# Layer-norm tiles before attention: each tile's PSUM evacuation issued after the next tile's Ln and Exp

## The chip, the cores and the metric

The kernel runs on all 8 cores of one Trainium2 chip, each with its own share of the rows and no exchange between cores. The metric is the device time of the slowest core in microseconds (us).

## What is computed

One transformer-like layer over x of shape 16 x 2048 x 1024 (batch, sequence, width), float32:

```python
x = x + layernorm(attention(layernorm(x), w_q, w_k, w_v, w_u, b_u))   # 16 heads of 64, causal
x = x + layernorm(ffn(layernorm(x), ...))    # a gated recurrence over the 16 batches, then tanh
```

`layernorm` subtracts the mean over the 1024 columns and divides by sqrt(variance + 1e-5); it has no weights. Attention needs K and V of all 2048 rows of a batch, and Q of the core's own rows only.

## The kernel before

Each core owns 256 of the 2048 rows of every batch (16 strips of 16 rows). For each of the 16 batches it computes the layer norm, K and V of the whole sequence, and Q, scores, softmax and output for its own 256 rows. After all batches the FFN part loads and transposes its weights, normalises the core's rows, runs the recurrence over the batches, and writes y.

The program is written by hand as one list of operations for each engine (class `Plan`): `P.op(engine, ...)` appends an instruction, `P.wait(engine, semaphore, value)` makes that engine wait at this place of its list, and `inc` raises a semaphore when an instruction ends. An engine works through its list in order, so the order in which the Python code calls `P.op` is the order on the engine.

A batch begins with the layer-norm stage: 16 tiles of 128 rows from xg (the whole sequence) into lnf, and then 2 tiles from xm (the core's own rows) into lnm, which is the buffer of. Each is one call of `emit_ln_tile_bf` (line 226). For tile k:

- SyncE loads the tile (512 KB) into a slot, once GpSimd has finished with that slot's last tile (lines 233 to 235). There are 4 slots for the xg tiles (two xt buffers, ex and of) and 2 for the xm tiles (the xt buffers).
- VectorE computes mean and variance (lines 242 to 248).
- ScalarE computes 1/sqrt(variance + eps) as Ln and then Exp (lines 251 and 254).
- GpSimd normalises the tile into lt or x1, in turn (line 258). It waits until TensorE has transposed the tile of two calls ago.
- TensorE transposes it in eight 128x128 pieces into one half of the PSUM buffer PA, in turn (line 265). It waits until the half's last tile has been evacuated.
- ScalarE copies that half as bfloat16 into lnf or of (line 272): the evacuation, counted by the semaphore ve_Tevac.

After the last tile of a batch TensorE waits for all evacuations (line 362) and starts the K projection (line 373), 32 groups of 8 matmuls, and then V (line 390), Q (line 416) and the attention proper. The two waits with a lag of one are these, as the code has them:

```python
P.wait("gpsimd", "te_T", max(P.v("te_T") - 1, 0))
P.wait("tensor", "ve_Tevac", max(P.v("ve_Tevac") - 1, 0))
```

`P.v` is the count of the increments written so far, at the place in the Python code where it is called.

Of the kernel before, what the change touches and what calls it, by code (L numbers as in the profile page):

```python
# [79 lines left out]
def _apof(buf):  # L80
    return buf.ap() if hasattr(buf, "ap") and callable(getattr(buf, "ap")) \
        else buf


def sub3(buf, off, d1, d2):
    a = _apof(buf)
    return bass.AP(a.tensor, a.offset + off, [[a.ap[0][0], a.ap[0][1]], d1, d2])
# [135 lines left out]
    return nm, rs  # L223


def emit_ln_tile_bf(P, B, src_dram_ap, k, dst_fm, dst_col, slots):
    nslot = len(slots)
    par4 = k % nslot
    par2 = k % 2
    xt = slots[par4]  # L230
    lt = B["lt"] if par2 == 0 else B["x1"]
    PA = B["PA"]
    P.wait("sync", "gp_lnapply", max(P.v("gp_lnapply") - (nslot - 1), 0))
    P.dma("sync", lambda sy: sy.dma_start(out=xt, in_=src_dram_ap),
          inc=f"ldx{par4}")
    P.wait("vector", "gp_lnapply", max(P.v("gp_lnapply") - (nslot - 1), 0))
    P.wait("vector", f"ldx{par4}")
    bnb, mv, nm, rs = (B["bnb"][par4], B["mv"][par4], B["nm"][par4],
                       B["rs"][par4])

    def stats(v):
        v.bn_stats(bnb[:, 0:6], xt[:, 0:512])  # L242
        return v.bn_stats(bnb[:, 6:12], xt[:, 512:1024])
    P.op("vector", stats, inc="ve")
    P.wait("vector", "ve")
    P.op("vector", lambda v: v.bn_aggr(mv[:], bnb[:]), inc="ve")
    P.wait("vector", "ve")
    P.op("vector", lambda v: v.tensor_scalar(nm[:], mv[:, 0:1], -1.0, None,
                                             ALU.mult), inc="ve")
    P.wait("scalar", "ve")  # L250
    P.op("scalar", lambda sc: sc.activation(rs[:], mv[:, 1:2], AF.Ln,
                                            bias=B["eps"][:, 0:1]), inc="se")
    P.wait("scalar", "se")
    P.op("scalar", lambda sc: sc.activation(rs[:], rs[:], AF.Exp, scale=-0.5),  # L254
         inc="ve_rs")
    P.wait("gpsimd", "ve_rs")
    P.wait("gpsimd", "te_T", max(P.v("te_T") - 1, 0))
    P.op("gpsimd", lambda g, lt=lt: g.tensor_scalar(  # L258
        lt[:], xt, nm[:, 0:1], rs[:, 0:1], ALU.add, ALU.mult),
        inc="gp_lnapply")  # L260
    P.wait("tensor", "gp_lnapply")
    P.wait("tensor", "ve_Tevac", max(P.v("ve_Tevac") - 1, 0))
    po = 1024 * par2
    for ch in range(8):
        P.op("tensor", lambda t, ch=ch, po=po, lt=lt: t.transpose(  # L265
            PA[:, po + 128 * ch: po + 128 * (ch + 1)],
            lt[:, 128 * ch:128 * (ch + 1)], B["identf"][:]),
            inc="te_T" if ch == 7 else None)
    P.wait("scalar", "te_T")
    stride = dst_fm.shape[1] // 8  # L270
    P.op("scalar", lambda sc, po=po, dst_col=dst_col, dst_fm=dst_fm, stride=stride:
         sc.copy(  # L272
             sub3(dst_fm, dst_col, [stride, 8], [1, 128]),
             sub3(PA, po, [128, 8], [1, 128])),
         inc="ve_Tevac")


def emit_ln_tile(P, B, src_dram_ap, par, dst_fm, dst_col, lt2=False):
# [35 lines left out]
def emit_attention(P, B, cfg):  # L314
    NB = DEBUG_NB or cfg["NB"]
    units = cfg["units"]
    xg, xm = cfg["xg"], cfg["xm"]
    lnf, kf, va, qf, ex, of = (B["lnf"], B["kf"], B["va"], B["qf"], B["ex"],
                               B["of"])
    wq, wk, wv, wu = B["wq"], B["wk"], B["wv"], B["wu"]  # L320
    PA, PB = B["PA"], B["PB"]
    lnm = lnf if cfg["lnm_is_lnf"] else B["lnm"]
    masks = B["masks"]

    for name, arena in (("wq", wq), ("wk", wk), ("wv", wv), ("wu", wu)):
        dram = cfg[name]
        for dmc in range(8):
# [6 lines left out]
          inc="ld_mask")  # L334
# [3 lines left out]
    for b in range(NB):  # L338
# [6 lines left out]
        if cfg.get("al_on_ex"):  # L345
# [6 lines left out]
            P.wait("sync", "st_al0")  # L352
            P.wait("sync", "st_al1")
        slots = cfg["ln_slots"]
        for tt in range(NKT):
            emit_ln_tile_bf(P, B, xg[b, 128 * tt:128 * (tt + 1), :], tt,
                            lnf, 128 * tt, slots)
        if not cfg["lnm_is_lnf"]:
            for tt in range(cfg["NQ"] // 128):
                emit_ln_tile_bf(P, B, xm[b, 128 * tt:128 * (tt + 1), :], tt,  # L360
                                lnm, 128 * tt, slots[0:2])
        P.wait("tensor", "ve_Tevac")
        P.wait("vector", "gp_lnapply")
        if DEBUG_STAGE == "ln1":
# [2 lines left out]
        for g4 in range(4):  # L367
            for hp in range(8):
                par = (g4 * 8 + hp) % 2
                po = 512 * par  # L370
                P.wait("tensor", "ve_kevac", max(P.v("ve_kevac") - 1, 0))
                for dmc in range(8):
# [5 lines left out]
                        inc="te_k" if dmc == 7 else None)  # L378
# [5 lines left out]
        for kt in range(NKT):  # L384
            par = kt % 2
            po = 1024 * par
            P.wait("tensor", "gp_vrepack", max(P.v("gp_vrepack") - 1, 0))
            for dmc in range(8):
                for hf in range(2):
# [6 lines left out]
                        inc="te_v" if (dmc == 7 and hf == 1) else None)  # L396
# [4 lines left out]
                inc="gp_vrepack")  # L401
# [6 lines left out]
        for unit in units:  # L408
# [3 lines left out]
            for hp in range(8):  # L412
                P.wait("tensor", "ve_qevac")
                for dmc in range(8):
# [8 lines left out]
                         inc="te_q" if dmc == 7 else None)  # L423
# [10 lines left out]
            for quad in range(4):  # L434
# [24 lines left out]
                for idx, (i, vs, d_lo, d_w) in enumerate(ktl):  # L459
                    slot = 1024 * (idx % 2)  # L460
                    P.wait("tensor", "se_exp", max(P.v("se_exp") - 1, 0))
                    for hq in range(4):
# [10 lines left out]
                             inc="te_s" if hq == 3 else None)  # L473
                    if d_w:
                        for hq in range(4):
# [8 lines left out]
                                 inc="te_s" if hq == 3 else None)  # L484
# [19 lines left out]
                for j in range(2):  # L504
# [5 lines left out]
                        inc="te_bc" if j == 1 else None)  # L510
# [5 lines left out]
                for hq in range(4):  # L516
# [6 lines left out]
                        inc="ve_norm")  # L523
# [3 lines left out]
            for st in range(2):  # L527
                po = 1024 * st
# [8 lines left out]
                for j in range(2):  # L537
# [5 lines left out]
                        inc="te_up" if j == 1 else None)  # L543
# [272 lines left out]
def build_attn_program(version):  # L816
# [17 lines left out]
    with ctx:  # L834
        B = alloc_common(nc, ctx, need_attn=True, need_ffn=False)
        B["masks"] = ctx.enter_context(
            nc.sbuf_tensor("masks_sb", [128, 8 * mask_w], BF16))
        P = Plan(nc, ctx)
        blk = ctx.enter_context(nc.Block())
        cfg = {  # L840
            "NB": NB, "NQ": NQ, "units": make_units(version),
            "xg": xg, "xm": None, "lnm_is_lnf": True,
            "wq": wq, "wk": wk, "wv": wv, "wu": wu, "bu": bu,
            "masks_dram": masks_dram, "mask_w": mask_w,
            "aln_dst": lambda b, r0: aln[b, r0:r0 + 128, :],
        }
        emit_setup(P, B)
        emit_attention(P, B, cfg)
        P.run(blk)
# [34 lines left out]
def build_fused_program():  # L884
# [20 lines left out]
    with ctx:  # L905
# [27 lines left out]
        })  # L933
        emit_setup(P, B)
        emit_attention(P, B, cfg_a)
        for eng in ENGINES:
            P.wait(eng, "st_al0")
# [100 lines left out]
```

## Time and profile before

| | us |
|---|---|
| median of the 2 timed runs | 7825.04 (7629.27 and 8020.81) |
| the profiled execution | 7630.95 |
| its span on the slowest core (core 5) | 7629.1 |
| spans of the 8 cores | 7609.1 to 7629.1 |
| batch 1: GpSimd's first tile to first K matmul | 416.13 to 509.79 |
| busy: PE, DVE, ACT, POOL | 62%, 29%, 19%, 5% |

PE is TensorE's matmuls, PEld its weight loads, DVE VectorE, ACT ScalarE, POOL GpSimd, SPq SyncE's queue, which issues the loads. L272 is line 272 of the kernel. Busy shares are means over stages of different kinds: the 16 batches take up to about 5490 us, the FFN part the rest.

### The profile page before, as it was taken

The page shows a single profiled execution, that of the slowest core. Times are in us where ns is not written, and L with a number is a line of the kernel's source. Part 1 is how long each engine was busy: PE and PEld are TensorE (multiplying, and loading weights), DVE is VectorE, ACT ScalarE, POOL GpSimd, SP SyncE. Part 2 cuts the span into 40 slices and gives each one's busy share as a digit, 9 for nine tenths or more (in the row PEclk, how much of TensorE's full clock was granted, in tenths as well). Part 3 has the DMA queues.
Part 4 walks back from the last instruction along what each step waited for, and adds up shares of the span by engine and source line. Part 5 has one row for each costly group of instructions (what it writes and reads, how often), then busy time and mean ns, then how long its engine had stood idle before and what let it go on. Part 6 is the DMA issues. An engine that isn't in the chain of part 4 may idle for free.

```text
span 7629.1 us, 84840 instructions; the slowest of 8 cores (7609.1 to 7629.1 us)
## 1 busy us (share of the span) xinstructions
PE 4743.2 (62%) x31972; PEld 3005.3 (39%) x31972; DVE 2205.7 (29%) x3874; ACT 1480.4 (19%) x2697; POOL 419.4 (5%) x367
## 2 busy tenths in 40 slices
PE   2856757585766758585775748586633216999322
PEld 1534344343434344343434434343411115888110
DVE  1232323222232322223232222223222233333334
ACT  1212130312212031221213031221200001222222
POOL 3010100101010000101010010101000010000000
PEclk9867768686877768686776868687755557999666
DMA  4010110101010010101011010101011221000222
GB/s 94 1 53 18 36 39 14 53 1 53 1 53 28 25 48 6 53 1 53 17 36 40 14 53 1 53 1 53 20 66 66 80 88 48 12 15 9 80 92 92
DMA packets 95066, 299.11 MB, mean 39 GB/s; under 512 B 14800, under 2 KB 14800, under 8 KB 94672
## 3 DMA queue, kind: packets, MB, share of 16 engines
q1 hardware_dynamic: 90000, 285.30, 11.3%
q0 software_dynamic: 4672, 8.39, 0.7%
q8 instruction: 267, 4.37, 0.2%
q14 instruction: 127, 1.04, 0.0%
HBM read 268.49 MB, written 33.55 MB: 40 GB/s over the span
## 4 chain that ended last, share of the span: by engine, by line
PE 56%; DVE 11%; issue 10%; ACT 10%; DMA 6%; POOL 5%; SPq 1%; ACTq 0%; DVEq 0%; POOLq 0%
PE PA L373 12%; PE PB L390 12%; PE PA L265 7%; PE PB L688 4%; PE PB L451 4%; PE PB L677 4%; ACT ex L487 3%; PE PB L416 3%; PE PA L467 2%; POOL x_ L258 2%; POOL lt L258 2%; PE PA L584 2%; DVE of L519 1%; PE PB L758 1%; PE PA L531 1%
## 5 line engine op out<-in xcount | busy, mean ns | idle before, releaser
L487 ACT ACTIVATE ex<-PA 128x1024 bf16<-128x1024 f32 (+15 forms) x1024 | 624.3, 624 | 2683.4 <-PE PA L477 2640.6
L373 PE MATMUL PA<-lnf,wk_sb 128*128 128x512 bf16 x4096 | 919.6, 389 | 22.2 <-ACT of L272 22.2
L390 PE MATMUL PB<-wv_sb,lnf 128*128 128x512 bf16 x4096 | 886.7, 379 | 0.0
L265 PE MATMUL PA<-identf,lt 128*128 128x128 f32 x1152 | 279.2, 424 | 723.0 <-POOL lt L258 644.9
L373 PEld LDWEIGHTS PA<-lnf,wk_sb 128*128 128x128 bf16 x4096 | 407.7, 100 | 532.6 <-issue 71.9
L451 PE MATMUL PB<-ex,va 128*65 128x256 bf16 (+15 forms) x4096 | 483.6, 243 | 208.2 <-ACT ex L487 131.2
L390 PEld LDWEIGHTS PB<-wv_sb,lnf 128*128 128x128 bf16 x4096 | 400.8, 98 | 483.3
L265 PE MATMUL PA<-identf,x_ 128*128 128x128 f32 x1152 | 279.3, 424 | 473.1 <-POOL x_ L258 473.1
L380 DVE CAST kf<-PA 128x512 bf16<-128x512 f32 x512 | 354.1, 692 | 707.0 <-PE PA L373 707.0
L265 PEld LDWEIGHTS PA<-identf,lt 128*128 128x128 f32 x1152 | 225.6, 223 | 777.5 <-issue 777.5
L467 PE MATMUL PA<-qf,kf 128*128 128x256 bf16 (+15 forms) x4096 | 515.2, 256 | 22.0 <-DVE qf L427 22.0
L398 DVE CAST va<-PB 128x1024 bf16<-128x1024 f32 x256 | 314.1, 1227 | 578.5 <-PE PB L390 578.5
L272 ACT CAST lnf<-PA 128x1024 bf16<-128x1024 f32 x256 | 259.1, 1012 | 1003.2 <-PE PA L265 1003.2
L265 PEld LDWEIGHTS PA<-identf,x_ 128*128 128x128 f32 x1152 | 225.7, 223 | 526.6 <-issue 526.6
L512 DVE CAST rb<-PB 64x1024 bf16<-64x1024 f32 x64 | 77.9, 1217 | 1162.1 <-PE PB L505 1162.1
L451 PEld LDWEIGHTS PB<-ex,va 128*65 128x65 bf16 x4096 | 304.5, 118 | 254.8 <-issue 238.4
L758 PE MATMUL PB<-wv_sb,va 128*128 128x512 bf16 x512 | 151.1, 468 | 374.0 <-DMA va<-ln2s 371.3
L584 PE MATMUL PA<-identf,xt 128*128 128x128 f32 x512 | 168.8, 433 | 333.3 <-DVE lnf L590 38.3
L467 PEld LDWEIGHTS PA<-qf,kf 128*128 128x128 bf16 x4096 | 329.1, 108 | 103.0 <-issue 67.8
L242 DVE BATCH_NORM_STATS2 bnb<-xt 128x6 f32<-128x512 f32 x160 | 111.1, 694 | 722.8 <-DMA xt<-xg 425.0
L258 POOL TENSOR_SCALAR lt<-xt,nm,rs 128x1024 f32<-128x1024 f32 x80 | 95.7, 1196 | 3995.2 <-ACT rs L254 3995.2
L416 PE MATMUL PB<-of,wq_sb 128*128 128x256 bf16 x1024 | 212.6, 378 | 151.8 <-DVE qf L427 125.0
(99 smaller groups left out, 4900.2 us busy)
## 6 DMA issues: line engine op xcount, KB each, us to landing
xt<-xg SPq DMA_DIRECT2D x128, 512.0 KB, 3.9
xt<-xm SPq DMA_DIRECT2D x96, 512.0 KB, 4.6
ex<-xg SPq DMA_DIRECT2D x64, 512.0 KB, 3.9
of<-xg SPq DMA_DIRECT2D x64, 512.0 KB, 3.9
va<-alns SPq DMA_DIRECT2D x64, 256.0 KB, 4.5
va<-ln2s SPq DMA_DIRECT2D x32, 512.0 KB, 3.7
y<-lt SPq DMA_DIRECT2D x32, 512.0 KB, 3.0
alns<-ex SPq DMA_DIRECT2D x32, 256.0 KB, 2.0
```

The lines of the kernel that those rows point to most:

```text
L258: P.op("gpsimd", lambda g, lt=lt: g.tensor_scalar(lt[:], xt, nm[:, 0:1], rs[:, 0:1], ALU.add, ALU.mult), inc="gp_lnapply")
L265: P.op("tensor", lambda t, ch=ch, po=po, lt=lt: t.transpose(PA[:, po + 128 * ch: po + 128 * (ch + 1)], lt[:, 128 * ch:128 * (ch + 1)], B[" ...
L373: P.op("tensor", lambda t, dmc=dmc, hp=hp, g4=g4, po=po: t.matmul(PA[:, po:po + 512], wk[:, 1024 * dmc + 128 * hp: 1024 * dmc + 128 * (hp ...
L380: P.op("vector", lambda v, hp=hp, g4=g4, po=po: v.tensor_copy(kf[:, 2048 * hp + 512 * g4: 2048 * hp + 512 * (g4 + 1)], PA[:, po:po + 512]) ...
L390: P.op("tensor", lambda t, dmc=dmc, kt=kt, hf=hf, po=po: t.matmul(PB[:, po + 512 * hf: po + 512 * (hf + 1)], lnf[:, 2048 * dmc + 128 * kt: ...
L398: P.op("vector", lambda v, po=po, kt=kt: v.tensor_copy(sub3(va, 1040 * kt, [65, 16], [1, 64]), sub3(B["PB"], po, [64, 16], [1, 64])), inc= ...
L416: src_stride=src_stride: t.matmul(PB[:, 1792:2048], wq[:, 1024 * dmc + 128 * hp: 1024 * dmc + 128 * (hp + 1)], lnm[:, src_stride * dmc + q ...
L451: last=(idx == nkt_u - 1): t.matmul(PB[0:65, 256 * hq + vs: 256 * (hq + 1)], va[:, 1040 * i + 65 * h: 1040 * i + 65 * (h + 1)], sub2(ex, 1 ...
L467: lambda t, i=i, vs=vs, hq=hq, hp=hp, qo=qo, slot=slot: t.matmul(PA[:, slot + 256 * hq + vs: slot + 256 * (hq + 1)], kf[:, 2048 * hp + 128 ...
L487: P.op("scalar", lambda s, vs=vs, slot=slot, idx=idx: s.activation(sub3(ex, 1024 * (idx % 2) + vs, [256, 4], [1, 256 - vs]), sub3(PA, slot ...
L584: P.op("tensor", lambda t, ic=ic, oc=oc: t.transpose(PA[:, 128 * oc:128 * (oc + 1)], B["xt"][oc][:, 128 * ic: 128 * (ic + 1)], identf[:]), ...
L677: par=par, first=(ic == 0 and gi in (0, 2)): t_.matmul(PB[:, doff:doff + 256], B[wT][:, 1024 * ic + 128 * mc: 1024 * ic + 128 * (mc + 1)], ...
```

## The change

`emit_ln_tile_bf` no longer writes tile k's evacuation at its end; it returns it as a function, and the call for tile k+1 writes it right after that tile's Exp. The last one of a batch is written after the loops. On ScalarE the order was Ln k, Exp k, evacuation k, Ln k+1, ...; it becomes Ln k, Exp k, evacuation k-1, Ln k+1, Exp k+1, evacuation k, and so on. The instructions themselves and the buffers are the same.

```diff
-def emit_ln_tile_bf(P, B, src_dram_ap, k, dst_fm, dst_col, slots):
+def emit_ln_tile_bf(P, B, src_dram_ap, k, dst_fm, dst_col, slots, pend=None):
...
     P.op("scalar", lambda sc: sc.activation(rs[:], rs[:], AF.Exp, scale=-0.5),
          inc="ve_rs")
+    if pend is not None:
+        pend()
     P.wait("gpsimd", "ve_rs")
...
-    P.wait("scalar", "te_T")
-    stride = dst_fm.shape[1] // 8
-    P.op("scalar", lambda sc, po=po, dst_col=dst_col, dst_fm=dst_fm, stride=stride:
-         sc.copy(
-             sub3(dst_fm, dst_col, [stride, 8], [1, 128]),
-             sub3(PA, po, [128, 8], [1, 128])),
-         inc="ve_Tevac")
+
+    def evac():
+        P.wait("scalar", "te_T")
+        stride = dst_fm.shape[1] // 8
+        P.op("scalar",
+             lambda sc, po=po, dst_col=dst_col, dst_fm=dst_fm, stride=stride:
+             sc.copy(
+                 sub3(dst_fm, dst_col, [stride, 8], [1, 128]),
+                 sub3(PA, po, [128, 8], [1, 128])),
+             inc="ve_Tevac")
+    return evac
...
+        pend = None
         for tt in range(NKT):
-            emit_ln_tile_bf(P, B, xg[b, 128 * tt:128 * (tt + 1), :], tt,
-                            lnf, 128 * tt, slots)
+            pend = emit_ln_tile_bf(P, B, xg[b, 128 * tt:128 * (tt + 1), :],
+                                   tt, lnf, 128 * tt, slots, pend)
         if not cfg["lnm_is_lnf"]:
             for tt in range(cfg["NQ"] // 128):
-                emit_ln_tile_bf(P, B, xm[b, 128 * tt:128 * (tt + 1), :], tt,
-                                lnm, 128 * tt, slots[0:2])
+                pend = emit_ln_tile_bf(P, B, xm[b, 128 * tt:128 * (tt + 1), :],
+                                       tt, lnm, 128 * tt, slots[0:2], pend)
+        if pend is not None:
+            pend()
         P.wait("tensor", "ve_Tevac")
```

evac()'s wait on te_T names a value when it is called: inside the call for tile k+1 and ahead of that tile's transposes, so it is the count up to tile k's own.

## Rows read from the trace of the kernel before

**Rows 1.** The page's chain that ended last, by line.
```profile
PE PA L373 12%; PE PB L390 12%; PE PA L265 7%; PE PB L688 4%; PE PB L451 4%; PE PB L677 4%; ACT ex L487 3%; PE PB L416 3%; PE PA L467 2%; POOL x_ L258 2%; POOL lt L258 2%; PE PA L584 2%; DVE of L519 1%; PE PB L758 1%; PE PA L531 1%
```

**Rows 2.** One window: length, busy us of PE, PEld, DVE, ACT, POOL; clock; DMA.
```profile
416.00:510.00 94.00, 35.11 (x145) 28.35 (x146) 27.91 (x68) 24.97 (x52) 21.48 (x18) 0.50 0.28 86
```

**Rows 3.** The evacuation's line over the whole run: count, shortest, median, longest ns.
```profile
L272 ACT CAST lnf<-PA x256: 1012/1012/1013, 80.1 to 5245.7; 128x1024 bf16<-128x1024 f32 x128
L272 ACT CAST of<-PA x32: 1012/1012/1012, 163.7 to 5256.2; 128x1024 bf16<-128x1024 f32 x32
```

**Rows 4.** Timeline, batch 1, one tile: start, us, instruction, idle before and releaser.
```profile
419.61 1.01 ACT L272 CAST lnf<-PA 128x1024 bf16<-128x1024 f32 x1 [3.71 <-PE PA L265]
...
420.52 0.30 ACT L251 ACTIVATE rs<-mv,eps 128x1 f32<-128x1 f32 x1
420.90 0.20 ACT L254 ACTIVATE rs<-rs 128x1 f32<-128x1 f32 x1
...
421.34 1.19 POOL L258 TENSOR_SCALAR x_<-xt,nm,rs 128x1024 f32<-128x1024 f32 x1 [4.01 <-ACT rs L254]
...
422.78 1.94 PE L265 MATMUL PA<-identf,x_ 128*128 128x128 f32 x8 [3.27 <-POOL x_ L258]
...
424.81 1.01 ACT L272 CAST lnf<-PA 128x1024 bf16<-128x1024 f32 x1 [3.71 <-PE PA L265]
...
426.55 1.19 POOL L258 TENSOR_SCALAR lt<-ex,nm,rs 128x1024 f32<-128x1024 f32 x1 [4.01 <-ACT rs L254]
```

**Rows 5.** Timeline, head of batch 1: the first tiles' statistics, the first Ln and normalise.
```profile
413.36 0.69 DVE L242 BATCH_NORM_STATS2 bnb<-xt 128x6 f32<-128x512 f32 x1 [7.04 <-DMA xt<-xg]
...
415.31 0.29 ACT L251 ACTIVATE rs<-mv,eps 128x1 f32<-128x1 f32 x1 [10.79 <-DVE nm L248]
...
415.89 0.69 DVE L242 BATCH_NORM_STATS2 bnb<-xt 128x6 f32<-128x512 f32 x1 [0.68 <-DMA xt<-xg]
416.13 1.19 POOL L258 TENSOR_SCALAR lt<-xt,nm,rs 128x1024 f32<-128x1024 f32 x1 [249.54 <-ACT rs L254]
...
417.77 0.69 DVE L242 BATCH_NORM_STATS2 bnb<-ex 128x6 f32<-128x512 f32 x1
```

**Rows 6.** Loads in batch 1: one load and its reader, landings, the window of four.
```profile
427.81 0.33 SPq L234 DMA_DIRECT2D ex<-xg  x1
...
431.71 0.69 DVE L242 BATCH_NORM_STATS2 bnb<-ex 128x6 f32<-128x512 f32 x1 [3.24 <-DMA ex<-xg]
...
DMA to landing us min/median/max: 3.6/3.8/8.5
...
412.00:416.00 4.00, 0.00 (x0) 0.00 (x0) 1.75 (x5) 0.50 (x2) 0.00 (x0) 0.50 1.01 281
```

**Rows 7.** Timeline, tail of batch 1: tile 14, the xm loads, last evacuation, K.
```profile
489.06 1.19 POOL L258 TENSOR_SCALAR lt<-ex,nm,rs 128x1024 f32<-128x1024 f32 x1 [4.01 <-ACT rs L254]
490.33 5.53 SPq L234 DMA_DIRECT2D xt<-xm  x2
...
494.23 0.69 DVE L242 BATCH_NORM_STATS2 bnb<-xt 128x6 f32<-128x512 f32 x1 [13.82 <-DMA xt<-xm]
...
508.43 1.01 ACT L272 CAST of<-PA 128x1024 bf16<-128x1024 f32 x1 [3.98 <-PE PA L265]
...
509.79 50.43 PE L373 MATMUL PA<-lnf,wk_sb 128*128 128x512 bf16 x220 [1.73 <-ACT of L272]
```

**Rows 8.** Timeline, batch 0: GpSimd on its second tile, and the K start.
```profile
81.79 1.19 POOL L258 TENSOR_SCALAR x_<-xt,nm,rs 128x1024 f32<-128x1024 f32 x1 [42.15 <-ACT rs L254]
...
170.02 10.16 PE L373 MATMUL PA<-lnf,wk_sb 128*128 128x512 bf16 x37 [1.25 <-ACT of L272]
```

**Rows 9.** Windows at the K start, PE only: length, busy (count), clock, DMA.
```profile
508.00:512.00 4.00, 2.27 (x7) 0.50 0.01 2
512.00:516.00 4.00, 4.00 (x12) 0.57 0.00 0
516.00:520.00 4.00, 4.00 (x20) 1.00 0.00 0
```

## What I expected, and why

> **What bounds the kernel now.** I read the page's chain first, then asked the trace which stretches that chain runs through, and then read one such stretch instruction by instruction. The chain by lines is led by matmuls of the K and V projections, but line 265 (the layer-norm transposes) stands third, and both forms of line 258 (GpSimd's normalise) are on it too [rows 1]. These lines exist in one stage only: the layer norm at the head of each batch. The window over one such stage shows what is to be seen there: of 94 us, TensorE is busy 35, VectorE 28, ScalarE 25, GpSimd 21 and the DMA engines 28% [rows 2]. No engine is near its limit, so the stage is bound by a chain that goes from engine to engine. It has 18 tiles a batch, 288 in all: the evacuation of line 272 ran 256 times into lnf and 32 times into of [rows 3].
>
> One tile, read in order of time [rows 4]: the evacuation of the tile before starts on ScalarE at 419.61; Ln follows at 420.52 (0.91 later), Exp at 420.90 (0.38), GpSimd's normalise at 421.34 (0.44), the eight transposes at 422.78 (1.44), and the next evacuation at 424.81 (2.03). That sums to 5.20 us and closes on itself, for GpSimd starts again at 426.55, 5.21 after 421.34. The evacuation sat idle 3.71 us before it started, waiting for TensorE. Ln of the next tile stands behind it in ScalarE's program, although VectorE had that tile's statistics long before: those of the tile that GpSimd starts at 426.55 were begun at 417.77 [rows 4, 5]. So each tile passes through all five stations before the next one may begin, and the stage costs 5.2 us a tile.
>
> **The change, part by part.** No instruction is added or removed. The evacuation of tile k-1 moves behind Ln and Exp of tile k on ScalarE; the last one of a batch is issued after the loop. The waits of the other engines keep their values: when tile k's own waits are written, the evacuations counted are again those up to k-1, so TensorE waits for evacuation k-2 (the half of PA it will overwrite), and GpSimd for the transposes of k-2 (the lt or x1 buffer it will overwrite). With both buffers in pairs, tile k no longer needs tile k-1.
>
> Steady state: evacuation k-1 is followed on ScalarE by Ln k+1, Exp k+1, GpSimd k+1, TensorE k+1, evacuation k+1. These are the same five steps, 0.91 + 0.38 + 0.44 + 1.44 + 2.03 = 5.20 us, but they now carry the chain forward by two tiles: 2.60 us a tile, if no engine is full before that. TensorE needs 1.94 us a tile [rows 4], ScalarE 0.91 + 0.38 + 0.20 = 1.5, GpSimd 1.2, VectorE 1.88 (from 415.89 to 417.77, two tiles' statistics back to back [rows 5]). All fit in 2.60. GpSimd and VectorE already run side by side in these rows with unchanged durations, so I put their overlap at nothing; the new overlap, an evacuation reading one half of PA while TensorE writes the other, I put at nothing too. The nearest row is the K projection, where VectorE reads one half of PA while TensorE writes the other and 20 matmuls still fall in 4 us at the full clock [rows 9]. Were the evacuation 10% longer by it, the nine two-tile steps of a batch would cost 0.9 us, 14 us in all; that is my upper bound, and below nothing there is no reason for a gain.
>
> Loads: a tile's slot is refilled four tiles ahead. Line 258 of tile k-4 starts, 1.26 later SyncE issues the load (426.55 to 427.81), and VectorE starts on it 3.90 after that (431.71) [rows 4, 6]; Ln can start 1.95 after the statistics begin (413.36 to 415.31 [rows 5]). Together 7.11 us after GpSimd's start on k-4. The new schedule wants that Ln at 2 x 5.21 - 0.82 = 9.60 us. So a load has 2.5 us to spare: it may take 6.4 us where it takes 3.90. The demand rises from one 512 KB load in 5.2 us to one in 2.6, about 200 GB/s; when four loads were queued at the head of the batch, the engines moved 281 GB/s at a share of 1.01 [rows 6], which is 1.87 us for one. The spacing of 2.6 is longer than that, so loads don't queue up. I take 3.90. The bounds are 3.6, the shortest landing of the batch, and 8.5, the longest, seen behind three others [rows 6].
>
> Head of the batch: tile 0 is unchanged, GpSimd at 416.13 [rows 5]. Tile 1's statistics begin at 415.89, so its Ln starts at 417.84 and GpSimd at 418.66, where it was 421.34. Evacuation 0 runs at 419.61 as before, and tile 2 follows at 421.34. Even tiles thus start at 416.13 + 5.21 j, tile 14 at 452.6 instead of 489.06 [rows 7]: 36.46 us earlier. Odd tiles run 2.52 behind the even ones.
>
> Tail: the two tiles from xm use only two slots, so their loads are issued late. Call T the start of GpSimd on tile 14. The load of the first is issued at T + 1.27 and its statistics begin at T + 5.17 (489.06, 490.33, 494.23 [rows 7]). In the old order that was hidden. Now Ln is wanted at T + 4.38 and can start only at T + 5.17 + 1.95 = 7.12: a stall of 2.7 us on ScalarE, with the evacuation of tile 15 queued behind it. That evacuation then runs at about T + 7.7 and ends before the transposes that need its half of PA, at T + 11.9, so it costs nothing more. The second load is issued after tile 15, at T + 2.52 + 1.27 = 3.79; statistics 7.69, Ln 9.64, GpSimd 10.46, transposes 11.90, evacuation 13.93. The first K matmul came 1.36 after the last evacuation (508.43 to 509.79), and that evacuation ran 0.28 later than the pattern; with both it starts at T + 15.57, where before it was T + 20.73. That gives 5.16 us.
>
> A batch gains 36.46 + 5.16 = 41.6 us of 93.7 (416.13 to 509.79). Batch 0 waits for weights until 78 us, but its second tile starts GpSimd at 81.79 and the first K matmul comes at 170.02 [rows 8]; in the new order it is tile 2 that starts there, tile 14 comes six steps later at 113.1 and K at 128.7: 41.3. The FFN stages have their own tile code and are not touched. 16 x 41.6 = 666 us. From the profiled execution's own 7630.95 us this gives **6965 us**. The median shown, 7825.04, is that of two runs at 7629.27 and 8020.81; my sum stands against the lower. Were the new kernel's median to lie 2.5% above its profiled execution in the same way, it would read 7142, which my range holds.
>
> **TensorE's clock.** In this stage the granted clock is 0.50, the level of 1.2 GHz, with TensorE busy 35 of 94 us on transposes alone [rows 2]. At the K projection's start it is still 0.50, then 0.57, and 1.00 from 516 on; the windows hold 7, 12 and then 20 matmuls in 4 us [rows 9]. From 509.79 to 516 some 30 could have run, 17 did, so the cold start costs about 2.6 us a batch. In the new order TensorE would be busy 1.94 of each 2.6 us. I leave the clock as it is, because all transposes seen in this stage ran at 0.50. The Trainium skill (TensorE: Matmul & The Clock Gate, Part 4: PE-mode transpose) says that transposes do not count as activity for the clock; by that rule the sum stays at 6965. The same page's Part 1 says that activity in general releases the throttle; if transposes did count, it would be the second rival below. The trace agrees with the first at 37% busy; no run here yet shows 75%.
>
> **Rivals.**
> *Loads become the bound.* If eight cores asking for twice the rate bring every load to 8.5 us, four tiles take 1.26 + 8.5 + 1.95 + 0.82 = 12.53 us instead of 10.41. Tiles 6, 10 and 14 each lose 2.12 (6.4 together), and the tail, where two slots serve, about 4.0: a batch gains 31.2, and the time is 7631 - 499 = 7132. For it: the queue of four loads did show 8.5. Against it: they were issued within 2 us, and three tiles' time between loads is now left free. 12%.
> *TensorE's clock rises.* Transposes would at best take half, 0.97 less in each two-tile step: seven steps and the tail are 7.8, with the K start 10.4 us a batch, so 6965 - 166 = 6799. For it: twice the density. Against it: nothing in the trace shows the transposes' duration at another clock, nor the clock rising under them. 10%.
> *It doesn't separate the tiles.* If some wait still tied tile k to k-1, the period would stay 5.2 and the time 7631. The pairs of buffers and the wait values speak against it. 4%.
> *Slower: head-of-line blocking on ScalarE.* Evacuation k now stands behind Ln k+1, which needs a load that the evacuation doesn't. The ScalarE queue is served in order, as the row at 420.52 right behind 419.61 shows. This loses once four tiles take more than 4 x 5.2 us, that is once a load takes over 20.8 - 4.0 = 16.8 us; at 20 us the 18 tiles would take 108 us for 94, and the time would be about 7631 + 16 x 14.5 = 7860. The longest load on record is half of the threshold. 2%.
>
> **How the numbers follow.** My forecast, 6965, holds 72%; by itself it spans 6920 (a K start without the cold matmuls) to 7020 (loads of 6.5 us, which add 2.6 in each tail, 42 in all, and the 14 us of the overlap). The range is 6880 to 7150: up to the load-bound case, down to half way to the case of the raised clock, which leaves out 16%. A difference of about 2% is what a measurement of this kernel can tell from none. All cases but the last two are faster by over 2%: faster 0.94, same 0.04, slower 0.02.
>
> **What would show it.** In the new profile, GpSimd's starts in a batch should alternate at 2.5 and 2.7 us; the evacuation's row should show an idle time well under 3.71; Ln and Exp should stand ahead of it; the first K matmul should come about 52 us after GpSimd's first tile. VectorE's wait for xt<-xm should appear on ScalarE as a wait of Ln, near 2.7 us. Landings much over 6.4 us, or VectorE as ScalarE's releaser in every tile, would mean the loads bind. Clock rows over 0.50 in the stage, or transposes under 1.94 us for eight, would mean the second rival. A spacing of 5.2 would mean that I overlooked a wait.

## The result, and the profile after

| | before | changed |
|---|---|---|
| median, us | 7943.36 (10 runs, 7629.27 to 8113.69) | 7077.54 (13 runs, 6943.50 to 7435.96) |
| runs with every core at its usual clock, us | 7629 to 7633 | 6943 to 6948 |
| ratio of these | | 0.9101, 95% interval 0.9083 to 0.9119 |

Some executions on this chip have four or eight cores at a lower granted clock and take some per cent longer, whatever the kernel, so the ratio goes by the others, and rows are always those of a core at its usual clock. For the changed kernel that is core 5, which is also the core of the rows before; its span is 6927.5 us where it was 7629.1. A second profile of the changed kernel (e11_again, below) gave 6947.8 for the same core.

The timeline of core 5 in batch 1, in the steady part (start, us, instruction, idle before and releaser), answers to [rows 4]:

```profile
404.77 1.19 POOL L260 TENSOR_SCALAR x_<-xt,nm,rs 128x1024 f32<-128x1024 f32 x1 [1.57 <-ACT rs L254]
...
405.48 1.01 ACT L277 CAST lnf<-PA 128x1024 bf16<-128x1024 f32 x1 [0.94 <-PE PA L267]
...
406.21 1.94 PE L267 MATMUL PA<-identf,x_ 128*128 128x128 f32 x8 [0.83 <-POOL x_ L260]
...
406.39 0.30 ACT L251 ACTIVATE rs<-mv,eps 128x1 f32<-128x1 f32 x1
...
406.78 0.20 ACT L254 ACTIVATE rs<-rs 128x1 f32<-128x1 f32 x1
407.21 1.19 POOL L260 TENSOR_SCALAR lt<-ex,nm,rs 128x1024 f32<-128x1024 f32 x1 [1.25 <-ACT rs L254]
408.25 1.01 ACT L277 CAST lnf<-PA 128x1024 bf16<-128x1024 f32 x1 [1.27 <-PE PA L267]
...
409.98 1.19 POOL L260 TENSOR_SCALAR x_<-of,nm,rs 128x1024 f32<-128x1024 f32 x1 [1.57 <-ACT rs L254]
```

GpSimd's starts are 2.44 and 2.77 us apart, two of them 5.21, where one took 5.21 before. The evacuation waits 0.9 to 1.3 us for TensorE instead of 3.71. Over the run its two rows, which answer to [rows 3], show an idle time of 301.5 + 43.4 us where it was 1003.2 + 120.1 (groups of ScalarE's instructions, core 5: count, busy us, mean ns, idle before; L272 is the evacuation in the kernel before, L277 in the changed one):

```profile
L272 ACT CAST lnf<-PA 128x1024 bf16<-128x1024 f32 x256 | 259.1, 1012 | 1003.2 <-PE PA L265 1003.2
L251 ACT ACTIVATE rs<-mv,eps 128x1 f32<-128x1 f32 x288 | 85.5, 297 | 148.4 <-DVE nm L248 148.3
...
L272 ACT CAST of<-PA 128x1024 bf16<-128x1024 f32 x32 | 32.4, 1012 | 120.1 <-PE PA L265 120.1
...
L277 ACT CAST lnf<-PA 128x1024 bf16<-128x1024 f32 x256 | 258.8, 1011 | 301.5 <-PE PA L267 301.2
L251 ACT ACTIVATE rs<-mv,eps 128x1 f32<-128x1 f32 x288 | 85.5, 297 | 234.0 <-DVE nm L248 233.9
...
L277 ACT CAST of<-PA 128x1024 bf16<-128x1024 f32 x32 | 32.4, 1012 | 43.4 <-PE PA L267 43.4
```

The evacuation waits 778 us less in all. Ln (L251) waits 86 us more for VectorE's statistics, 234.0 for 148.4 (3.96 us in the tail of batch 1 alone, below). The difference, 693 us, is close to what the stages became shorter by, 685 us (below).

The same timeline at the tail of batch 1 answers to [rows 7]:

```profile
407.21 1.19 POOL L260 TENSOR_SCALAR lt<-ex,nm,rs 128x1024 f32<-128x1024 f32 x1 [1.25 <-ACT rs L254]
...
408.48 3.09 SPq L234 DMA_DIRECT2D xt<-xm  x2
...
413.71 0.69 DVE L242 BATCH_NORM_STATS2 bnb<-xt 128x6 f32<-128x512 f32 x1 [6.91 <-DMA xt<-xm]
...
415.66 0.29 ACT L251 ACTIVATE rs<-mv,eps 128x1 f32<-128x1 f32 x1 [3.96 <-DVE nm L248]
...
416.16 0.99 ACT L277 CAST lnf<-PA 128x1024 bf16<-128x1024 f32 x1
...
416.48 1.19 POOL L260 TENSOR_SCALAR lt<-xt,nm,rs 128x1024 f32<-128x1024 f32 x1 [5.31 <-ACT rs L254]
...
421.83 1.01 ACT L277 CAST of<-PA 128x1024 bf16<-128x1024 f32 x1 [0.86 <-PE PA L267]
...
423.09 2.10 PE L382 MATMUL PA<-lnf,wk_sb 128*128 128x512 bf16 x9 [1.63 <-ACT of L277]
```

The first xm load is issued 1.27 us after GpSimd's start on tile 14, and Ln waits 3.96 us for its statistics: the stall that the prediction put at 2.7. The evacuation at 416.16 is that of tile 15: it stands behind this Ln and Exp in ScalarE's list, 2.8 us after its transposes had ended (at 413.36), and it costs nothing, as the prediction had it.

From such timelines I read, for each of the 16 batches, when GpSimd starts on tiles 0, 14, 16 and 17 and when the first K matmul starts. The table gives means over batches 1 to 15 in us (tile 16 is the first xm tile). "Fast" is how many of a batch's 18 groups of eight transposes took under 1.5 us. Rows are of core 5, but of core 1 for e1_xm4, core 0 for e2_before_xm4 and core 2 for e7_fill4. Between cores and between executions of one kernel the column "0 to K" differs by about 0.4 us: core 0 of the kernel before has 94.09, and core 5 in e11_again 51.18.

| kernel | tile 0 to 14 | 14 to 16 | 14 to K | 0 to K | fast |
|---|---|---|---|---|---|
| before | 73.15 | 10.45 | 20.50 | 93.65 | 0 |
| changed | 35.01 | 8.09 | 15.76 | 50.77 | 2.7 |
| predicted | 36.47 | 7.94 | 15.57 | 52.0 | 0 |
| e1_xm4 | 35.25 | 5.16 | 12.40 | 47.64 | 2.7 |
| e2_before_xm4 | 73.26 | 10.48 | 20.88 | 94.14 | 0 |
| e3_tied | 43.51 | 7.99 | 16.16 | 59.67 | 0 |
| e4_depth2 | 30.91 | 4.53 | 10.78 | 41.70 | 8.7 |
| e5_slots2 | 55.86 | 8.01 | 16.51 | 72.36 | 0 |
| e6_before_slots2 | 73.15 | 10.46 | 20.48 | 93.63 | 0 |
| e7_fill4 | 32.94 | 7.81 | 15.15 | 48.09 | 15.3 |
| e8_depth2_s8 | 26.65 | 3.81 | 9.73 | 36.38 | 14.2 |
| e10_before_fill4 | 66.08 | 9.20 | 18.29 | 84.37 | 11.0 |

The whole sum closes on this table: core 5 spends 1536.5 us from tile 0 to K in the 16 batches before, 851.4 after, 685.1 less; the 15 stretches from a K start to the next tile 0 give another 11 (245.51 to 244.75 each); together 696 of the 701.6 by which its span fell. Nothing was given back elsewhere. In e11_again the same core spends 857.6 us from tile 0 to K, 679 less than before, and 245.80 in each stretch between: the gain in the stages repeats, the 11 us outside them doesn't.

### The profile page after: what moved, and what is told of

Its sections match the earlier page's. It is cut to its first block, busy times and chain, and to the rows that moved or that the text cites. A ratio compares the mean times of both kernels' runs of the same rounds, so it can differ in the third digit from the quotient of the medians.

```text
span 7069.1 us, 84840 instructions; the slowest of 8 cores (6927.5 to 7069.1 us)
## 1 busy us (share of the span) xinstructions
PE 4839.7 (68%) x31972; PEld 3022.9 (43%) x31972; DVE 2205.7 (31%) x3874; ACT 1485.6 (21%) x2697; POOL 420.0 (6%) x367
## 4 chain that ended last, share of the span: by engine, by line
PE 58%; DVE 13%; ACT 9%; issue 8%; DMA 8%; POOL 3%; SPq 1%; DVEq 0%; ACTq 0%; POOLq 0%
PE PA L382 14%; PE PB L399 13%; PE PB L697 5%; PE PB L460 5%; PE PB L686 4%; PE PA L267 4%; ACT ex L496 3%; PE PB L425 3%; PE PA L476 3%; PE PA L593 2%; PE PA L540 1%; DVE of L528 1%; PE PB L767 1%; POOL x_ L260 1%; DMA xt<-xg 1%
## 5 line engine op out<-in xcount | busy, mean ns | idle before, releaser
L382 PE MATMUL PA<-lnf,wk_sb 128*128 128x512 bf16 x4096 | 973.2, 405 | 22.0 <-ACT of L277 22.0
L399 PE MATMUL PB<-wv_sb,lnf 128*128 128x512 bf16 x4096 | 946.5, 397 | 0.0
L267 PE MATMUL PA<-identf,lt 128*128 128x128 f32 x1152 | 256.8, 398 | 463.9 <-POOL lt L260 372.9
L267 PEld LDWEIGHTS PA<-identf,lt 128*128 128x128 f32 x1152 | 208.4, 209 | 515.3 <-issue 515.3
L277 ACT CAST lnf<-PA 128x1024 bf16<-128x1024 f32 x256 | 258.8, 1011 | 307.9 <-PE PA L267 307.6
L644 PE MATMUL PA<-identf,lt 128*128 128x128 f32 x256 | 62.1, 424 | 314.5 <-POOL lt L637 314.5
```

Of the source, the lines that this page charges most:

```text
L267: P.op("tensor", lambda t, ch=ch, po=po, lt=lt: t.transpose(PA[:, po + 128 * ch: po + 128 * (ch + 1)], lt[:, 128 * ch:128 * (ch + 1)], B[" ...
L382: P.op("tensor", lambda t, dmc=dmc, hp=hp, g4=g4, po=po: t.matmul(PA[:, po:po + 512], wk[:, 1024 * dmc + 128 * hp: 1024 * dmc + 128 * (hp ...
L399: P.op("tensor", lambda t, dmc=dmc, kt=kt, hf=hf, po=po: t.matmul(PB[:, po + 512 * hf: po + 512 * (hf + 1)], lnf[:, 2048 * dmc + 128 * kt: ...
```

## The experiments

**Is the stall in the tail the late load?** The xm tiles get all four slots, so their loads wait for a tile four back, as the others do.

```diff
-                                       tt, lnm, 128 * tt, slots[0:2], pend)
+                                       tt, lnm, 128 * tt, slots, pend)
```

> The changed kernel, with the two xm tiles loaded under the same rule as the others: the slot is free four tiles back, so the first xm load is issued after tile 12 and not after tile 14. Chain theory (the stall that the changed kernel shows in its tail, 8.1 us from GpSimd's tile 14 to its tile 16 where a steady pair takes 5.2, is the late load): that pair takes 5.2 to 5.3, the first K matmul comes about 13 us after tile 14 instead of 15.8, a gain of 2.5 to 3 us in each of 16 batches, 40 to 48 us, ratio to the kernel before near 0.904. Rival (the tail is bound by ScalarE or by GpSimd, the load only happens to be late as well): no change, ratio 0.910.

Measured: ratio 0.9026 (0.9004 to 0.9048), under the changed kernel's by more than both intervals. Core 1's GpSimd rows at the tail of batch 1:

```profile
409.06 1.20 POOL L260 TENSOR_SCALAR lt<-ex,nm,rs 128x1024 f32<-128x1024 f32 x1 [1.45 <-ACT rs L254]
411.62 1.19 POOL L260 TENSOR_SCALAR x_<-of,nm,rs 128x1024 f32<-128x1024 f32 x1 [1.36 <-ACT rs L254]
414.27 1.19 POOL L260 TENSOR_SCALAR lt<-xt,nm,rs 128x1024 f32<-128x1024 f32 x1 [1.46 <-ACT rs L254]
```

From tile 14 to tile 16 it is 5.21 us, the steady pair, and the stall is gone. The batch gains 3.1 us. The same edit in the kernel before:

> The kernel before, with the same earlier xm loads. Chain theory: in the old order Ln of the first xm tile waited for the evacuation anyway (statistics ready at 496.1, Ln at 498.65), so the load is hidden: ratio 1.00, GpSimd's starts stay 5.2 apart up to the last tile. Rival (late xm loads always cost, before too): about 2.5 us a batch less, ratio 0.995.

Measured: ratio 1.0035 (0.9979 to 1.0092), GpSimd's pair at the tail 10.48 us on core 0, as on core 0 of the kernel before. The late load cost nothing in the old order, and it became a cost only when the chain that hid it was halved.

**Do the two PSUM halves carry the overlap?** TensorE waits for the evacuation just before, not for the one two back.

```diff
-    P.wait("tensor", "ve_Tevac", max(P.v("ve_Tevac") - 1, 0))
+    P.wait("tensor", "ve_Tevac")
```

> The changed kernel, but TensorE waits for the evacuation of the tile just before (as if PA had one half only). Theory that the pair of PSUM halves lets two tiles overlap: from the end of one tile's transposes 0.09 us to the evacuation, 1.0 to 1.4 until TensorE may start, 1.94 for the transposes, so 3.1 to 3.4 us a tile in place of 2.6; 18 tiles cost 9 to 14 us more a batch, 150 to 230 us in all, ratio 0.93 to 0.94. Rival (only ScalarE's order matters, the halves don't): ratio 0.910.

Measured: ratio 0.9304 (0.9273 to 0.9334). The timeline of core 5, batch 1:

```profile
390.00 1.01 ACT L277 CAST lnf<-PA 128x1024 bf16<-128x1024 f32 x1 [1.68 <-PE PA L267]
...
391.15 1.94 PE L267 MATMUL PA<-identf,lt 128*128 128x128 f32 x8 [1.25 <-ACT lnf L277]
...
393.18 1.01 ACT L277 CAST lnf<-PA 128x1024 bf16<-128x1024 f32 x1 [1.69 <-PE PA L267]
...
394.34 1.94 PE L267 MATMUL PA<-identf,x_ 128*128 128x128 f32 x8 [1.25 <-ACT lnf L277]
```

TensorE is now released by the evacuation in each tile, and a tile takes 3.19 us in the steady part: 1.15 from the evacuation's start to the transposes, 1.94 for them and 0.09 back. The order on ScalarE alone gives most of the gain (ratio 0.9304), but not 2.6 us a tile. That takes the wait with a lag of one as well.

**Does the chain's length divide by the number of tiles in it?** Each evacuation is held back by two tiles, on top of e1_xm4 (the end of the batch writes both that are left).

```diff
-    if pend is not None:
-        pend()
+    if pend is not None and len(pend) == 2:
+        pend.pop(0)()
...
-    P.wait("tensor", "ve_Tevac", max(P.v("ve_Tevac") - 1, 0))
+    P.wait("tensor", "ve_Tevac")
...
+    te_val = P.v("te_T")
+
     def evac():
-        P.wait("scalar", "te_T")
+        P.wait("scalar", "te_T", te_val)
```

> As e1_xm4, but each evacuation is held back by two tiles: on ScalarE Ln k, Exp k, evacuation k-2. The five-step chain of 5.2 us then carries three tiles, 1.74 us each, so that another thing binds: VectorE 1.88, TensorE 1.94 at the lower clock, the load path (7.11 + 0.82)/4 = 1.98. Chain theory: 2.0 us a tile, the first K matmul 39 to 41 us after tile 0 instead of 50.8, 150 to 190 us in all, ratio 0.885 to 0.89. Load rival (loads land at 4.5 us or later under this rate): 2.1 to 2.3 a tile, ratio 0.89 to 0.895. Clock rival (denser transposes hold the clock at 1.00): eight transposes take 1.06 and TensorE doesn't bind, VectorE or the loads do, 1.9 to 2.0 a tile, and the K projection starts without cold matmuls.

Measured: ratio 0.8895 (0.8873 to 0.8916). A tile takes 2.2 us (30.91 / 14), the load rival's value, and the rows of core 5 say the same: VectorE waits for the load, and Ln for VectorE.

```profile
376.40 0.69 DVE L242 BATCH_NORM_STATS2 bnb<-xt 128x6 f32<-128x512 f32 x1 [1.30 <-DMA xt<-xg]
...
378.35 0.29 ACT L251 ACTIVATE rs<-mv,eps 128x1 f32<-128x1 f32 x1 [1.67 <-DVE nm L248]
...
378.85 0.99 ACT L279 CAST lnf<-PA 128x1024 bf16<-128x1024 f32 x1
```

The evacuation hardly waits any more, 56.6 + 22.0 us over the run for 301.5 + 43.4, and Ln waits for VectorE 364.6 us for 233.9. The chain moved on from ScalarE's order to the load path. The clock rival holds in part as well: 8.7 of 18 groups of transposes were fast.

**How long is the load path?** Two slots for all tiles, in both kernels.

```diff
-        slots = cfg["ln_slots"]
+        slots = cfg["ln_slots"][0:2]
```

> The changed kernel with two slots for all tiles instead of four, so that a load is issued only after GpSimd has finished the tile two back. Load-path theory (1.26 + 3.9 + 1.95 + 0.82 = 7.93 us from GpSimd's start on tile k-2 to its start on tile k): 3.97 us a tile, tile 14 at 55.5 us after tile 0 (35.0 with four slots), ratio 0.95 to 0.96. Rival (loads are prefetched well enough anyway, ScalarE's chain of 5.2 us for two tiles binds): ratio 0.910.

Measured: ratio 0.9558 (0.9530 to 0.9586), tile 0 to 14 in 55.86 us for 55.5 expected. In the timeline of core 5 the same slot comes round every 7.7 us, with the statistics waiting for the load each time:

```profile
400.67 1.19 POOL L260 TENSOR_SCALAR lt<-xt,nm,rs 128x1024 f32<-128x1024 f32 x1 [4.92 <-ACT rs L254]
...
408.40 1.19 POOL L260 TENSOR_SCALAR lt<-xt,nm,rs 128x1024 f32<-128x1024 f32 x1 [4.00 <-ACT rs L254]
...
413.38 0.69 DVE L242 BATCH_NORM_STATS2 bnb<-xt 128x6 f32<-128x512 f32 x1 [3.08 <-DMA xt<-xg]
...
416.15 1.19 POOL L260 TENSOR_SCALAR lt<-xt,nm,rs 128x1024 f32<-128x1024 f32 x1 [3.74 <-ACT rs L254]
```

> The kernel before with two slots for all tiles. The load path of 7.93 us for two tiles lies under the old chain's 10.4, so the loads stay hidden: GpSimd's starts stay 5.2 apart, ratio 1.00. Together with e5_slots2 it tells that the load path was always there and only the new order uncovers it. Rival (two slots cost by themselves, through contention or issue): a ratio over 1.005 here.

Measured: ratio 0.9994 (0.9932 to 1.0056). With two slots the old order has 10.4 us for a path of 7.9 and loses nothing, the new one has 5.2 and loses 22 us a batch. With four slots the new order leaves the path 10.4 us.

**What does the clock do?** Four matmuls more per tile, which compute nothing that is used.

```diff
             inc="te_T" if ch == 7 else None)
+    for _ in range(4):
+        P.op("tensor", lambda t: t.matmul(
+            B["PB"][:, 0:512], B["wk"][:, 0:128], B["wk"][:, 0:512],
+            start=True, stop=True, skip_group_check=True))
```

> The changed kernel with four extra bf16 matmuls of 512 columns after each tile's transposes, into a part of PB that nothing reads; they only keep TensorE busy (1.7 us a tile at the clock of 0.50, 0.85 at 1.00). Clock theory (the transposes take 1.06 us at the higher level, as the changed kernel shows in some tiles): all tiles after the first two or three take 1.06, a pair of tiles 4.34 instead of 5.21, tile 14 at 31 us instead of 35.0, and the K projection starts without cold matmuls; 5 to 7 us less a batch, ratio 0.895 to 0.90. Rival (the fast transposes come from something else, the clock stays at 0.50 in the stage): TensorE is then busy 3.6 us a tile and binds, 3.6 a tile, ratio 0.945 to 0.95.

Measured, without an interval: the fastest execution took 6883.3 us, 0.902 of the 7625 to 7635 that the kernel before took beside it. In the windows of core 2, batch 1 (length, busy of PE, PEld, DVE, ACT, POOL, granted clock, DMA share, GB/s), the clock rises once and stays:

```profile
376.00:380.00 4.00, 3.23 (x12) 2.38 (x13) 3.43 (x10) 1.70 (x4) 1.71 (x2) 0.50 0.54 143
380.00:384.00 4.00, 4.00 (x22) 3.13 (x22) 2.90 (x7) 1.62 (x5) 1.25 (x2) 0.70 0.60 186
384.00:388.00 4.00, 3.51 (x23) 2.11 (x21) 2.09 (x7) 2.77 (x6) 2.34 (x2) 1.00 0.51 167
```

15 of 18 groups took about 1.06 us, as expected, but tile 0 to 14 fell by 2.1 us only, where I had expected 4, and the ratio is at 0.902 where I had expected 0.895 to 0.90. Some pairs of tiles do take the 4.34 us expected; between them a load is late again, as in e4_depth2, and Ln waits for it (timeline of core 2):

```profile
395.48 0.69 DVE L242 BATCH_NORM_STATS2 bnb<-xt 128x6 f32<-128x512 f32 x1 [1.88 <-DMA xt<-xg]
...
397.43 0.29 ACT L251 ACTIVATE rs<-mv,eps 128x1 f32<-128x1 f32 x1 [1.18 <-DVE nm L248]
```

Would the clock be worth more where nothing else is near? The next one puts the same matmuls into the kernel before:

> The kernel before, its order unchanged, with four extra bf16 matmuls of 512 columns after each tile's transposes, into a part of PB that nothing reads. Clock theory (busier TensorE raises the clock, eight transposes then take 1.06 us and not 1.94, in the old chain too): GpSimd's starts 4.3 us apart instead of 5.2 once the clock is up, about 15 us a batch less and a K start with few cold matmuls, 17 us in all, 270 us over 16 batches, ratio 0.96 to 0.97. Rival (the clock doesn't rise, because TensorE still stands idle between tiles): ratio 1.00, the extra matmuls being hidden in TensorE's 3.27 us of idle time.

Measured, without an interval: the fastest execution took 7445.74 us, 0.976 of the 7627 to 7630 beside it. The rival falls, and the clock theory holds in kind but not in size (0.96 to 0.97 expected): the rise doesn't last. The stage gives 9.3 us a batch, and the stretch from the K start on another 3.6 (241.92 us for 245.51): over the first 7 us of the K projection in batches 1 to 9 the granted clock is 0.81 to 1.00, with 28 to 34 matmuls, where the kernel before has 0.60 to 0.81 and 20 to 27. The windows of core 5, batch 1, with columns as above:

```profile
428.00:432.00 4.00, 1.93 (x12) 1.22 (x12) 1.23 (x4) 1.41 (x3) 0.86 (x2) 1.00 0.44 131
432.00:436.00 4.00, 2.97 (x12) 1.61 (x12) 1.65 (x4) 1.39 (x3) 0.78 (x1) 0.70 0.41 131
436.00:440.00 4.00, 2.44 (x11) 1.99 (x11) 1.65 (x4) 0.29 (x2) 1.19 (x1) 0.50 0.37 106
```

and GpSimd's rows of the timeline over the same stretch:

```profile
427.25 1.19 POOL L258 TENSOR_SCALAR lt<-ex,nm,rs 128x1024 f32<-128x1024 f32 x1 [3.15 <-ACT rs L254]
431.58 1.19 POOL L258 TENSOR_SCALAR x_<-of,nm,rs 128x1024 f32<-128x1024 f32 x1 [3.14 <-ACT rs L254]
436.25 1.19 POOL L258 TENSOR_SCALAR lt<-xt,nm,rs 128x1024 f32<-128x1024 f32 x1 [3.48 <-ACT rs L254]
441.46 1.19 POOL L258 TENSOR_SCALAR x_<-xt,nm,rs 128x1024 f32<-128x1024 f32 x1 [4.01 <-ACT rs L254]
```

With the transposes at 1.06 us, GpSimd starts every 4.33 us, at 1.94 every 5.21. 11 of 18 groups were fast. So the higher level is worth 0.88 us in each step of the chain that holds a group of transposes, in either order.

**Are the loads what binds at a depth of two?** On top of e4_depth2, four more slots, in kf, which is free until the K projection, and eight sets of the small statistics buffers for four.

```diff
+        ln_slots += [B["kf"].ap()[:, 2048 * i:2048 * (i + 1)].bitcast(F32)
+                     for i in range(4)]
```

> As e4_depth2 with eight slots: four more in kf, which is free until the K projection. In e4_depth2 a tile takes 2.2 us and VectorE waits for loads. Load theory: with loads issued eight tiles ahead only their rate counts (1.87 us for 512 KB at 281 GB/s) beside VectorE's 1.88: 1.9 us a tile, tile 14 at 27 us instead of 30.9, 3.5 to 4.5 us less a batch, ratio 0.88 to 0.883. Rival (TensorE at the lower clock, 1.94, or the rate of the loads under all eight cores binds at 2.1 or more): ratio 0.886 to 0.89.

Measured, without an interval: the fastest execution took 6690.85 us, 0.877 of the 7625 to 7635 beside it. Tile 0 to 14 takes 26.65 us, 1.90 a tile, so the load theory holds. GpSimd's starts on core 5 are 1.88 apart, VectorE's time for one tile's statistics:

```profile
379.66 1.20 POOL L260 TENSOR_SCALAR lt<-xt,nm,rs 128x1024 f32<-128x1024 f32 x1 [0.69 <-ACT rs L254]
381.54 1.19 POOL L260 TENSOR_SCALAR x_<-xt,nm,rs 128x1024 f32<-128x1024 f32 x1 [0.68 <-ACT rs L254]
```

Two things changed beside the slots. The small buffers were not what VectorE waited for in e4_depth2: there it waited 231 us for loads from xg and 4 us for GpSimd. And more transposes were fast, 14.2 of 18 for 8.7; at 1.94 us each they would have held a tile at 1.94 us, so by this estimate the clock bears on the last 0.04 us only.

It was timed again in more rounds, and so was the changed kernel:

> The same kernel as e8_depth2_s8, timed in more rounds for an interval. From its trace (16 stages of 36.4 us from the first normalise to the first K matmul, 50.8 in the changed kernel) I expect 16 x 14.4 = 230 us under the changed kernel and some 30 more from K projections that start at the higher clock: ratio to the kernel before 0.876 to 0.880.

Measured: ratio 0.8741 (0.8686 to 0.8795), four of the seven executions at 6684 to 6692 us; I had expected 0.876 to 0.880, and the interval ends just below the upper of these. This is the fastest version here, 3.7% under the changed kernel (6688 against 6946). Between its tiles the stage is bound by an engine, VectorE, and no longer by a chain.

> The changed kernel once more, unedited. If the gain belongs to the order on ScalarE and the level of all times to the session, the ratio repeats (0.908 to 0.912) whatever the two medians are. Rival (the gain depends on the session's level): a ratio outside 0.905 to 0.915.

Measured: ratio 0.9069 (0.8976 to 0.9161). The interval holds the values of both theories and can't tell them apart. The fastest executions can: 6944.70 us (at first 6943.50) over 7626.77 is 0.9106. The median was 7044.04. The kernel before had medians of 7943.36, 7640.65, 7721.69 and 7780.87 in four sessions, with its fastest always between 7625 and 7630.

## Why the prediction was right in its chain, and wrong in its level and in the clock

**The chain.** Right. The five steps now carry two tiles, 5.21 us; e3_tied ties each tile to the one before at TensorE and gets 3.19 us a tile. The 1.74 us that three tiles in the chain would give was never reached: e4_depth2 stopped at 2.2 for the loads and e8_depth2_s8 at 1.90 for VectorE. Tile 0 to 14 took 35.01 us for 36.47 predicted. The missing 1.5 us are the fast transposes. The even tiles go through seven steps of 5.21 us, and a group of an even tile that takes 1.06 us instead of 1.94 makes one step 0.88 shorter. In the batch shown (rows below) the groups of tiles 4 and 6 are such: 36.47 - 2 x 0.88 = 34.71, and the stretch took 34.72 us (372.49 to 407.21). The same working for each of batches 1 to 15 gives 34.82 in the mean for 35.01 measured. The 0.2 us between them stay open.

**Overlap.** Put at nothing, and rightly: the evacuation takes 1011 ns in the mean for 1012, and the transposes at 406.21 still take 1.94 us, though an evacuation (405.48 to 406.49) runs into them.

**Head.** Tile 1 follows tile 0 after 1.88 us in most batches, not 2.52: the second load landed sooner than in the batch that I read, and VectorE's own time set the distance. By the working above it cost or gave nothing, as the even tiles set the end.

**Loads.** Right that they don't bind: the median landing rose from 3.9 us to between 4.2 and 4.8 (the profile pages' loads from xg, changed kernel and e11_again), under the 6.4 allowed. The path of 7.93 us for two slots was measured at 7.98 (55.86 / 7) by e5_slots2.

**Tail.** Right in kind: 15.76 us for 15.57, with a stall of Ln for the xm load, 3.96 us in the batch shown where I had 2.7, since that load took 5.2 us from issue to the first reading and not 3.9. The gain in the tail was 4.74 us (20.50 to 15.76) and not 5.16. e1_xm4 removed the stall.

**TensorE's clock.** "I leave the clock as it is" was wrong, in the direction of the second rival. Windows of core 5, batch 1, in which TensorE does nothing but transposes:

```profile
380.00:384.00 4.00, 2.96 (x14) 2.25 (x12) 2.77 (x6) 2.36 (x5) 1.86 (x2) 0.56 0.67 209
384.00:388.00 4.00, 2.13 (x16) 1.72 (x16) 2.18 (x7) 2.48 (x7) 2.05 (x3) 1.00 0.53 175
388.00:392.00 4.00, 2.50 (x15) 2.33 (x16) 2.93 (x6) 2.20 (x6) 2.05 (x3) 0.79 0.82 246
```

and the transposes themselves, from the timeline:

```profile
381.02 1.94 PE L267 MATMUL PA<-identf,x_ 128*128 128x128 f32 x8
384.35 1.07 PE L267 MATMUL PA<-identf,lt 128*128 128x128 f32 x8 [1.39 <-POOL lt L260]
386.23 1.06 PE L267 MATMUL PA<-identf,x_ 128*128 128x128 f32 x8 [0.81 <-POOL x_ L260]
388.69 1.06 PE L267 MATMUL PA<-identf,lt 128*128 128x128 f32 x8 [1.40 <-POOL lt L260]
390.56 1.94 PE L267 MATMUL PA<-identf,x_ 128*128 128x128 f32 x8 [0.81 <-POOL x_ L260]
```

The granted clock goes from 0.50 to 1.00, that is from 1.2 to 2.4 GHz, after TensorE had transposed four tiles nearly back to back in pairs, and falls again after three fast ones. Here the rule of the Trainium skill that I had followed (TensorE: Matmul & The Clock Gate, Part 4: PE-mode transpose, by which transposes don't count for the clock) and the trace differ, and the measurement decides: transposes alone, here of float32 where that page measured bf16, raised it. The rival's price, 7.8 us a batch in the steps and the tail, was too high, since it assumed that the clock would stay up. Only 2.7 of 18 groups were fast, and only those of the even tiles count: 1.65 us a batch, 25 us over the 15 batches of the table. My sum had this term at nothing.

**The sum.** 666 us predicted, 685 and 679 found on core 5 in the stages, and 7631 - 666 = 6965 against 6946 for the fastest executions, 0.3% off; as a ratio 0.9127 against 0.9101. That it is so close is in part luck: tile 0 to 14 gave 38.14 us for 36.46, because of the clock, and the tail 4.74 for 5.16, because of the late load, so two misses of opposite sign met. Of the rivals, loads as the bound and tiles that don't separate didn't occur; e5_slots2 shows the first as it would have looked. Head-of-line blocking did occur once a batch, at the tail's Ln, and cost nothing.

**The level.** This is the step that failed, with the clock beside it. I took 7630.95, one profiled execution, as the level to subtract from, and gave the distance from it to the median of runs 2.5%, on the strength of two runs. The median of ten was 4.1% above it (7943.36), and that of the changed kernel 1.9% above its 6946, so the distance isn't one number for both. Put on that median, the measured ratio is 7229 us, outside my 6880 to 7150; the changed kernel's own median, 7077.54, lies inside it, 65 us below the 7142 that I gave for it. e11_again shows that this part moves with the session: the medians of one and the same kernel before ranged over 4%, the fastest executions over 0.1%. The range should have been wide enough for the level that two runs 5% apart left open, or should have said which level it was of.

What is still open: why the clock falls again after a few fast groups in the changed kernel and in e10_before_fill4, and stays up for most of the stage in e7_fill4 and e8_depth2_s8. The traces show it, no run here tells its rule.

## What to carry to other kernels

When no engine is busy over 40% in a stage, write down the loop of steps that one tile goes round and how many tiles it carries; an engine that serves its list in order makes that number one as soon as a late step of tile k stands ahead of an early step of tile k+1. Moving that step behind divides the period, if the buffers and the lags of the waits allow for it, and each division uncovers the next thing that was hidden: here a load issued late for two tiles, then the load path, then VectorE. Look for what is hidden by less than the time that you are about to remove, and mend it in the same go.

## What the runs showed of the hardware that I had not expected

Eight float32 transposes of 128x128 take 1.94 us at a granted clock of 0.50 and 1.06 at 1.00, and transposes alone can raise the clock from the one to the other. It rose for a few groups a batch in the changed kernel (2.7 of 18), for none in e3_tied, e5_slots2 and the kernel before, for about half in e4_depth2 (8.7), and for most of the stage in e8_depth2_s8 (14.2). A few matmuls whose result nobody reads made the stage of the kernel before 9.3 us shorter per batch (84.37 for 93.65) without any other edit; by the fastest execution that is 0.976 of the whole time.
